# Decay differences of a Mamba-2 scan: from a broadcast load and GpSimd to small matmuls into PSUM, with second copies of the chunk's buffers

## The reference

```python
x = L0_attn_hidden_states                    # (8, 2048, 2048), one row of the batch per core
xn = _layernorm(x, axis=-1)
x = x + attn(xn) + ffn(xn)

def attn(h):                                 # Mamba-2, 64 heads of 64, state 128
    zxbcdt = h @ in_proj_w.T
    z, xBC, dt = split(zxbcdt, [4096, 4096 + 4352])
    x, B, C = split(silu(causal_conv4(xBC) + conv_b), [4096, 4096 + 128])
    dt = clip(softplus(dt + dt_bias), 0, 100);  X = x * dt;  A = -exp(A_log) * dt
    # in chunks: A_cum = cumsum(A), L = exp(A_cum[l] - A_cum[s]) for s <= l
    Y_diag = einsum('bcln,bcsn,bhcls,bcshp->bclhp', C, B, L, X)
    states = einsum('bcln,bhcl,bclhp->bchpn', B, exp(A_cum[-1] - A_cum), X)
    Y_off  = einsum('bcln,bchpn,bhcl->bclhp', C, prev_states, exp(A_cum))
    y = Y_diag + Y_off + x * D
    return (norm_w * rms(y) * silu(z)) @ out_proj_w.T

def ffn(x):                                  # 8 experts of 1024, the two best by a gate
    ...
```

## Time and profile before

| what | us |
|---|---|
| three runs: median | 6566.19 |
| three runs: lowest, highest | 6562.95, 6885.02 |
| profiled execution | 6560.14 |
| span of its slowest core (core 1) | 6558.6 |
| phase B on that core, about | 4170 to 5975 |

### The profile page before, as it was taken

How to read it: one execution, slowest core, us unless ns; L and a number is a source line. 1 busy time by engine, 2 the same in 40 slices (tenths; PEclk the granted TensorE clock), 3 DMA queues, 4 the chain that set the end, 5 groups by cost and what they waited for, 6 DMA issues and landing times.

```text
span 6558.6 us, 49581 instructions; the slowest of 8 cores (6483.5 to 6558.6 us)
## 1 busy us (share of the span) xinstructions
PE 3836.6 (58%) x18408; PEld 1772.1 (27%) x18408; DVE 2122.1 (32%) x2645; ACT 618.5 (9%) x744; POOL 560.8 (9%) x292
## 2 busy tenths in 40 slices
PE   3437777777777777778998888311212112120799
PEld 3312333333323333333443333110101111110344
DVE  4521111111111111110005555555555555551211
ACT  2200000000000000001110000111111111110000
POOL 0000000000000000000000000112121212120000
PEclk6558888888888888889998888655555555555899
DMA  1134444444544444444323334222121212126343
GB/s 60 46 44 50 57 56 56 56 54 53 80 53 53 53 53 53 53 71 87 74 59 52 52 52 53 58 65 71 58 78 52 84 50 86 50 74 135 86 133 115
DMA packets 592959, 430.70 MB, mean 66 GB/s; under 512 B 482625, under 2 KB 549570, under 8 KB 576210
## 3 DMA queue, kind: packets, MB, share of 16 engines
q0 software_dynamic: 374048, 186.99, 23.9%
q1 hardware_dynamic: 218674, 240.53, 11.9%
HBM read 538.39 MB, written 76.06 MB: 94 GB/s over the span
## 4 chain that ended last, share of the span: by engine, by line
PE 45%; DMA 23%; DVE 15%; issue 8%; ACT 3%; POOL 2%; another core or an unknown queue 2%; SPq 2%; DVEq 0%; ACTq 0%; POOLq 0%
DMA wupb<-wupT 14%; PE pb L1083 14%; PE pb L1043 9%; PE pb L962 7%; PE pb L365 6%; PE pb L398 5%; DMA ygt<-ygs 4%; DVE cacc L418 2%; DMA gscr<-stk 2%; DVE Rq L734 2%; ACT Mq L737 2%; DMA Rq<-acr 2%; DVE y L766 1%; DVE P L836 1%
## 5 line engine op out<-in xcount | busy, mean ns | idle before, releaser
L1043 PE MATMUL pb<-xnTb,wupb 128*128 128x512 bf16 x4096 | 934.1, 389 | 661.4 <-DMA wupb<-wupT 660.8
L1083 PE MATMUL pb<-wd,h 128*128 128x512 bf16 x4096 | 898.8, 380 | 24.9 <-DVE h L1063 24.9
L1043 PEld LDWEIGHTS pb<-xnTb,wupb 128*128 128x128 bf16 x4096 | 402.1, 100 | 1193.2 <-issue 753.4
L398 PE MATMUL pb<-xnTb,wx 128*128 128x512 bf16 x2176 | 569.2, 431 | 117.1 <-DVE xbcin L407 117.1
L1063 DVE TENSOR_TENSOR h<-h,srow 128x1024 bf16<-128x1024 bf16 x128 | 88.6, 692 | 1519.3 <-ACT h L1056 1519.3
L962 PE MATMUL pb<-wo,ygc 128*128 128x512 bf16 x2048 | 444.9, 381 | 152.8 <-DVE wo L922 152.8
L1083 PEld LDWEIGHTS pb<-wd,h 128*128 128x128 bf16 x4096 | 394.8, 98 | 511.8 <-issue 47.4
L779 PE MATMUL pb<-XD,id 128*128 128x512 bf16 x128 | 59.7, 619 | 791.3 <-DVE y L766 791.3
L1104 DVE SCALAR_TENSOR_TENSOR acc<-pb,acc 128x512 bf16<-128x512 f32 x448 | 309.9, 692 | 480.4 <-PE pb L1083 480.4
L365 PE MATMUL pb<-wz,xnTb 128*128 128x512 bf16 x2048 | 444.5, 380 | 29.4 <-DMA wz<-winT 25.2
L1056 ACT ACTIVATE h<-pb,bupc_s 128x512 bf16<-128x512 f32 x256 | 175.9, 687 | 2259.2 <-PE pb L1043 2259.2
(11 more groups left out here) (133 smaller groups left out, 2707.0 us busy)
## 6 DMA issues: line engine op xcount, KB each, us to landing
wd<-wdT POOLq DMA_DIRECT2D x16, 4096.0 KB, 30.2
wupb<-wupT POOLq DMA_DIRECT2D x128, 512.0 KB, 7.6
Rq<-acr SPq DMA_DIRECT2D x64, 1024.0 KB, 6.7
wx<-winT POOLq DMA_DIRECT2D x34, 512.0 KB, 6.6
xt<-x SPq DMA_DIRECT2D x16, 1024.0 KB, 5.1
wz<-winT POOLq DMA_DIRECT2D x8, 2048.0 KB, 19.7
zs<-z SPq DMA_DIRECT2D x128, 128.0 KB, 1.8
xts<-xt SPq DMA_DIRECT2D x32, 512.0 KB, 3.8
```

The lines of the kernel that those rows point to most:

```text
L398: last = e.matmul(pb[bi][:, :], wb[:, :].rearrange("p (k c) -> p k c", k=KT)[:, k], self.xnTb[:, :].rearrange("p (k t) -> p k t", k=KT)[:, ...
L1043: last = e.matmul(pb[bi][:, :], wb[:, :].rearrange("p (k c) -> p k c", k=KT)[:, k], self.xnTb[:, :].rearrange("p (k t) -> p k t", k=KT)[:, ...
L1083: last = e.matmul(pb[bi][:, :], h16[:, j * HT + lt * 128: j * HT + (lt + 1) * 128], wd16[:, :].rearrange("p (j d) -> p j d", j=8)[:, j, ds ...
```

## The change

Only `phaseB` is edited, with one more input (`negHE`) and another shape of the scratch `acr`. What it does:

- The difference between the running sum at token l (on columns) and at token s (on partitions) is made by TensorE in PSUM. The running sum is split into three bf16 planes that add up to it, `asplit` (three copies and two subtractions on VectorE, 64 x 128 each), and heads 32 to 63 of it are copied to partitions 0 to 31 (`aB`, a sixth small operation). `acr` is stored as these three planes.
- For each quarter SyncE loads 3 x 2048 bf16 (12 KB) to one partition, `arow3`, a single buffer. For each of four groups of 512 columns, TensorE runs six matmuls into bank 2 or 3: three with the row of ones on `arow3` (depth 1) and three with `asplit` or `aB` on `negHE` (depth 32). VectorE clamps the group from PSUM into `Dq`. ScalarE then exponentiates the quarter as before. `Rq`, its 1 MB loads and the GpSimd subtraction are gone.
- Banks: transposes and small products share banks 0 and 1, the differences take 2 and 3, and `yoff`, `yd` and `st` of both halves take 4 to 7.
- `stk`, `atok`, `dstok`, `eatok`, `Xc`, `Xd` and `yg16` get second copies, taken in turn by chunk. `zc` gets a single one, loaded at the start of its own chunk, behind the next chunk's `xtc`.
- The debug switch `sec`, which is not set, is removed.

```diff
-        zc = [self.sb(f"zc{b}", [128, I4], BF16, pbs) for b in range(2)]
+        zc = self.sb("zc", [128, I4], BF16, pbs)
-        Rq = [self.sb(f"Rq{b}", [128, 16 * CH], F32, pbs) for b in range(2)]
+        Dq = [self.sb(f"Dq{b}", [128, 16 * CH], F32, pbs) for b in range(2)]
+        negHE = self.sb("negHE_s", [32, 32 * CH], BF16, pbs)
+        arow3 = self.sb("arow3", [1, 3 * 16 * CH], BF16, pbs)
+        asplit = self.sb("asplit", [NH, 3 * CH], BF16, pbs)
+        aB = self.sb("aB", [32, 3 * CH], BF16, pbs)
...
             em.op("dve", ... stk[64:128, :] = stk[0:NH, :] - stk[0:NH, CH - 1:CH])
+            em.op("dve", ... asplit[:, 0:CH] = stk[0:NH, :])
+            em.op("dve", ... rres = stk[0:NH, :] - asplit[:, 0:CH])
+            em.op("dve", ... asplit[:, CH:2 * CH] = rres)
+            em.op("dve", ... rres = rres - asplit[:, CH:2 * CH])
+            em.op("dve", ... asplit[:, 2 * CH:3 * CH] = rres)
+            em.op("dve", ... aB[:, :] = asplit[32:64, :])
             em.op("sp", lambda e, c=c: e.dma_start(
-                self.acr_h[c].rearrange("(h l) -> h l", h=NH), stk[0:NH, :]),
-                reads=[r_stk], writes=[self.r_acr[c]], dma=True, dbg=f"acr{c}")
+                self.acr_h[c].rearrange("i (h l) -> h i l", h=NH),
+                asplit[:, :].rearrange("p (i l) -> p i l", i=3)),
+                reads=[r_asp], writes=[self.r_acr[c]], dma=True, dbg=f"acr{c}")
...
-                    em.op("sp", lambda e, c=c, q=q, rb=rb: e.dma_start(
-                        rb[:, :],
-                        bass.AP(self.acr_h.tensor, c * NH * CH + q * 16 * CH,
-                                [[0, 128], [1, 16 * CH]])),
-                        reads=[self.r_acr[c]], writes=[r_rb], dma=True,
-                        dbg=f"Rq{c}_{q}")
-                    em.op("pool", lambda e, q=q, rb=rb: e.tensor_tensor(
-                        ... ALU.subtract),
-                        reads=[r_rb, r_atok], writes=[r_rb], dbg=f"D{c}_{q}")
-                    em.op("dve", lambda e, rb=rb: e.tensor_scalar(
-                        rb[:, :], rb[:, :], 0.0, None, ALU.min),
-                        reads=[r_rb], writes=[r_rb], dbg=f"Dc{c}_{q}")
+                    em.op("sp", lambda e, c=c, q=q: e.dma_start(
+                        arow3[:, :].rearrange("o (i l) -> o i l", i=3),
+                        bass.AP(self.acr_h.tensor,
+                                c * 3 * NH * CH + q * 16 * CH,
+                                [[0, 1], [NH * CH, 3], [1, 16 * CH]])),
+                        reads=[self.r_acr[c]], writes=[r_arow], dma=True,
+                        dbg=f"ar{c}_{q}")
+                    for ssl in range(4):
+                        bk = 2 + ssl % 2
+                        cs = slice(ssl * 512, (ssl + 1) * 512)
+                        def dmm(e, q=q, cs=cs, bk=bk):
+                            last = None
+                            for i in range(3):
+                                last = e.matmul(
+                                    pb[bk][:, :], self.ones16[0:1, 0:128],
+                                    arow3[:, i * 2048:(i + 1) * 2048][:, cs],
+                                    start=(i == 0), stop=False)
+                                lhs = (asplit[0:32, i * CH:(i + 1) * CH]
+                                       if q < 2 else
+                                       aB[:, i * CH:(i + 1) * CH])
+                                last = e.matmul(
+                                    pb[bk][:, :], lhs,
+                                    negHE[:, (q % 2) * 2048:][:, cs],
+                                    start=False, stop=(i == 2))
+                            return last
+                        em.op("pe", dmm, reads=[r_arow, self.r_ones16,
+                              r_negHE, r_asp, r_aB], writes=[r_pb[bk]])
+                        em.op("dve", lambda e, cs=cs, bk=bk, db_=db_:
+                              e.tensor_scalar(
+                              db_[:, cs], pb[bk][:, :], 0.0, None, ALU.min),
+                              reads=[r_pb[bk]], writes=[r_db])
...
-                pbank_h = [pb[4 * half + i] for i in range(4)]     # yoff, yd and st
+                pbank_h = [pb[4 + i] for i in range(4)]
```

More of the change, by code:

```diff
@@ L572, in phaseB @@
         r_btok = em.res()
-        grow = self.sb("grow", [1, NH], F32, pbs)
-        r_grow = em.res()
         self.gscr_h = self.dint("gscr", [NCH, NH], F32)
         r_gscr = [em.res(f"g{c}") for c in range(NCH)]
+        self.negHE_h = self.din("negHE", [32, 32 * CH])
+        em.op("pool", lambda e: e.dma_start(negHE[:, :], self.negHE_h),
+              writes=[r_negHE], dma=True)
         em.op("dve", lambda e: e.memset(onesf[:, :], 1.0), writes=[r_onesf])
@@ L602, in phaseB @@
             xb, r_xb = xtc[bi], r_xtc[bi]
-            zb, r_zb = zc[bi], r_zc[bi]
+            stk, r_stk = stkb[bi], r_stkb[bi]
+            atok, r_atok = atokb[bi], r_atokb[bi]
+            dstok, r_dstok = dstokb[bi], r_dstokb[bi]
+            eatok, r_eatok = eatokb[bi], r_eatokb[bi]
+            yg16, r_yg = yg16b[bi], r_ygb[bi]
+            Xc, r_Xc = Xcb[bi], r_Xcb[bi]
+            Xd, r_Xd = Xdb[bi], r_Xdb[bi]
             if c + 1 < NCH:
@@ L646, in phaseB @@
+            em.op("act", lambda e, eatok=eatok, atok=atok: e.activation(
+                eatok[:, :], atok[:, :], AF.Exp),
+                reads=[r_atok], writes=[r_eatok], dbg="eatok")
+            em.op("sp", lambda e, c=c, stk=stk: e.dma_start(
                 self.gscr_h[c:c + 1, :].rearrange("o h -> h o"),
@@ L746, in phaseB @@
                         reads=[r_mb, r_Gm], writes=[r_mb], dbg=f"M{c}_{q}")
-                hsl = slice(half * 2048, (half + 1) * 2048)
-                pbank_h = [pb[4 * half + i] for i in range(4)]
-                r_pbh = [r_pb[4 * half + i] for i in range(4)]
+                pbank_h = [pb[4 + i] for i in range(4)]
+                r_pbh = [r_pb[4 + i] for i in range(4)]
                 def yoff(e, c=c, half=half, pbank_h=pbank_h):
@@ L835, in phaseB @@
                     em.op("dve", lambda e, n=n, sl2=sl2, pbank_h=pbank_h:
-                        e.tensor_tensor(
-                        P32[:, sl2], P32[:, sl2], pbank_h[n][:, :], ALU.add),
-                        reads=[r_pbh[n], r_P32], writes=[r_P32],
-                        dbg=f"Pa{c}_{half}_{n}")
+                          e.tensor_tensor(
+                          P32[:, sl2], P32[:, sl2], pbank_h[n][:, :], ALU.add),
+                          reads=[r_pbh[n], r_P32], writes=[r_P32],
+                          dbg=f"Pa{c}_{half}_{n}")
                 em.op("dve", lambda e, half=half: e.tensor_copy(
@@ L867, in phaseB, with tryg @@
                 pv = pb[bi2][:, :].bitcast(BF16)
-                def tryg(e, g=g, pv=pv):
+                def tryg(e, g=g, pv=pv, yg16=yg16):
                     last = None
@@ L1439, in shared_weights @@
     w["bdn"] = asc(np.asarray(inputs["L0_ffn_bdown"], f32))
+    he = np.zeros((32, 32, 128), f32)
+    for h in range(32):
+        he[h, h, :] = -1.0
+    w["negHE"] = asc(he.reshape(32, 32 * 128))
     w["idf"] = np.eye(128, dtype=f32)
```

243 lines of the change are left out of this document (124 added, 119 removed).

## The result

The kernel is slower. Its median is 6876 us (6824 to 7241, ten runs) against 6560 us (6546 to 6929, ten runs) before; the ratio is 1.0425, with an interval from 1.0408 to 1.0442, so some 279 us. The forecast was 6680, 120 us more than before. The rival "the clock stays low" had named 6886.

What follows compares the result with a forecast made beforehand. Phase B was taken as a chain of waits with no engine full; 5.5 us for the stretch plus 2.0 for the banks, 7.5 us a chunk times 16, added 120 to 6560, giving 6680 us, range 6595 to 6900.

Steps and rivals of the forecast that it cites:

- the clock stays low: Rival: thin matmuls don't raise TensorE's clock in phase B; 20.4 us a chunk, +326, 6886 us; chance 0.13.
- Which clock: Phase B quarters: clock falls at each `arow3` gap; 0.50 lasts 4.5 us in quarter 0, 3.5 in quarters 1 and 3.
- Matmul time: A quarter's 24 difference matmuls: columns set the time, 10.3 us at the low clock, 5.3 at the high.
- quarter 0: First quarter of a chunk, from the first `arow3` issue: 2.7 us landing plus matmuls, ending at 10.3 us.
- quarter 1: Second quarter, after the previous quarter's last matmul: load lands at 2.8, last 12 matmuls end at 9.8 us.
- quarter 2: First quarter of the second half: a bank waits behind VectorE's four additions; ends 19.0 us after quarter 1.
- end of the half: Clamp, exponential, products and closing matmuls after a half's last quarter, until VectorE starts adding: 12.3 us with waits.
- sum: Stretch from the first `arow3` issue to the second half's additions: 61.2 us against 55.7, 5.5 us longer a chunk.
- high-clock rival: Rival: clock stays high through phase B's load gaps; 2.8 us a chunk, +45, 6605 us; chance 0.10.
- Landing of `arow3`: Each quarter's small load in phase B lands in 2.7 us, with bounds 1.9 and 4.8.
- Banks: Half 0's `st` now shares banks 4 to 7 with the additions and waits for them: 2.0 us a chunk.
- The rival of the drains: Rival: each turn from 1-row to 32-row matmuls costs 0.1 us; 8.4 us a chunk, 6814 us; chance 0.10.

Runs made afterwards that it cites:

- e10: Against after: all 96 difference matmuls of a chunk padded with zero rows to 96 rows; 6730 us in one run, not compared.
- e1: Against after: all 96 difference matmuls of a chunk made 128 rows deep, added rows adding zero; 6628 to 6638 us, 1.0114 of the kernel before the change.
- after: The kernel with the whole change, against the kernel before it; median 6876 us against 6560, ratio 1.0425.
- e2: Against after: the 1-row difference matmuls padded with zero rows, so that all 96 are 32 rows deep; 6851 us in one run.
- e3: Against after: all 96 difference matmuls of a chunk made 64 rows deep; 6817 us.
- e6: Against after: one line undone, so the state matmuls of half 0 use banks 0 to 3 again; 6814.5 us.
- e4: Against after: `Rq` loads, GpSimd subtraction and clamp from SBUF restored, `acr` float32 again, bank plan and buffers kept; 6597.8 and 6600.9 us.
- e9: Against after: six difference matmuls stacked into one, next quarter's clamps under the exponential, differences and half-0 `st` in banks 0 to 3; 6372, 6379 and 6434 us.
- e5: Against after: two `arow3` buffers, one for each quarter of a half, with `Xd` and `yg16` single again; 6828.7 us.
- e7: Against after: the edits of e1, e5 and e6 together in one kernel; 6715.9 us, not compared.

## Why the prediction was wrong

The step that failed is under *Which clock*: I let a burst of the new matmuls raise the clock after 3.5 to 4.5 us, as the bursts of the earlier trace rows do. The terms that it mis-sized are the matmul times of the quarters. Both rows on which I leaned, the 64-column burst too, are 128 rows deep. The sentence under *Matmul time*, "No row has a 1-row matmul; columns set the time of all that are shown", held for the pace, 0.427 us for 512 columns at 0.50, and misled for the clock: a burst of the same columns raised it at 96 and 128 rows (e10, e1) and did not at 1, 32 and 64 (after, e2, e3), where it was high only behind 128-row products. What the burst is made of inside TensorE that the clock answers to stays open. My "against" in the low-clock rival varied the wrong size: columns, where the change varies rows. The Trainium skill ("TensorE: Matmul & The Clock Gate", What's actually happening) has the clock follow how busy TensorE has been recently and does not speak of depth; here TensorE was busy for 15.4 us on end and the clock stayed at 0.50.

Term by term, the ends of the quarters from the chains (us):

| term | forecast | low-clock rival | after | e1 |
|---|---|---|---|---|
| quarter 0 | 10.3 | 13.1 | 14.3 | 11.7 |
| quarter 1 | 9.8 | 13.1 | 12.9 | 8.8 |
| quarter 2 | 19.0 | 22.5 | 22.3 | 18.7 |
| quarter 3 | 9.8 | 13.1 | 12.9 | 8.8 |
| end of the half | 12.3 | 12.3 | 12.1 | 12.1 |
| sum | 61.2 | 74.1 | 74.5 | 60.1 |

- *The mechanism of the sum held.* With the clock as assumed (e1) 60.1 came for 61.2, without it 74.5 for 74.1. That e1 comes so close is in part luck, since inner choices were off against each other: in e1's chunk the clock did not fall at the gaps (quarters 1 and 3 each 1.0 shorter, close to the 8.9 of the high-clock rival), though it did behind at least 14 of that core's 32, while in quarter 0 the load landed in 3.5 us, not 2.7, and the clock rose after 5.4 us, not 4.5. In 14 chunks of this core it rose 2.9 to 5.9 us into quarter 0, with 4.6 in the middle, so the 4.5 was well chosen. In after, too, a quarter 0 that was 1.2 longer than the rival's is mostly made up by the other four terms.
- *Landing of `arow3`.* 2.7 was taken; the repeats landed in 2.2, the first of a chunk in 3.75. Within the bounds, and their mean over the three that count is 2.7.
- *Banks.* 2.0 forecast; 1.6 in the chain, 2.0 in the period by e6, which ran once. Right.
- *Hidden work.* VectorE's preparation of this chunk ends at 4443.9, with the row below from its timeline, and the first load lands at 4445.6: it stayed covered, as forecast, with 1.7 us to spare.

```profile
4443.19 0.68 DVE L730 TENSOR_TENSOR Xd<-Xc,dstok 128x512 bf16<-128x512 bf16 x1
```

- *Ahead of the stretch.* I counted the `gscr` store as unchanged; it waits 8.4 us instead of 10.0. Why was not tested. Together: 18.8 for the stretch, 1.6 for the banks, 1.6 off for `gscr`, 18.8 of the 19.8 us; the last 1.0 has no row.
- *The rivals.* The low clock, which I gave 0.13, is what came: it named 20.4 us a chunk and 19.8 were measured. The rival of the drains falls: the pitch between 1-row and 32-row matmuls is the plain 0.427, and e2 without any change of depth is not faster.
- *Where the expected 120 us became 316 in phase B.* Of 19.8 us a chunk, 13.4 go with the clock (e1 against after), 2.0 are the banks (e6), and 0.7 is what e4 keeps beside the banks. The rest, 3.7, is by subtraction what 96 matmuls and their loads cost over the `Rq` path even with e1's clock.

## What to carry to other kernels

Before moving work onto TensorE in many small matmuls, look in the trace for a burst of the same depth in rows, not only of the same columns, and price it at the low clock as long as none is found at the high one. Products that sum into one PSUM group can be stacked along the rows: 6 matmuls became one here. That, with two loads a chunk issued ahead in place of four, was worth 20.4 us a chunk (129.3 to 108.9), more than the clock. And ask what the engine that reads PSUM stands waiting for: reordering the clamps, with the banks of e9, was worth another 12.8 us a chunk, some 2.3 of them by the earlier state update, where the faster load (e5) gave 3.0 and then met that wait.

## What the runs showed of the hardware

- A burst of matmuls of 1, 32 or 64 rows did not bring the granted clock from 0.50 to 1.00 by itself, though TensorE was busy throughout: 10.4 us (15.4 us at 1 and 32 rows in e5). The same bursts with 96 or 128 rows, the added ones adding zero, brought it to 1.00 (5.4 us into the burst in e1's chunk above).
- A clock that 128-row products had raised let 512-column matmuls of 1 and 32 rows run at 0.22 us each, 12 of them at most before it was 0.50 again; at 64 rows up to 28.
- Depth costs nothing by itself: 0.427 us a matmul of 512 columns at 1, 32, 64, 96 and 128 rows, all at 0.50.
- The clock stayed at 1.00 over a gap of 2.48 us in the chunk of e1 shown, and fell 0.7 us after the end of an idle stretch of 3.42 us in e7. On core 3 of e1 at least 14 of 32 gaps of about 2.5 us were followed by a fall within 1.3 us. The length of the gap alone does not say which.
- In the chunks read, the same 12 KB load landed in 2.2 us when repeated (after) and in 3.4 to 4.1 us as the first of a chunk, with the broadcast of `gscr` issued ahead of it (3.75 in after, 3.53 in e1, 4.09 in e5, 3.37 in e7).
